# A graph layer's edge MLP: the ring of finished rows and scatter indices goes from four sets to eight

## The chip, the cores and the metric

The kernel runs on one core of a Trainium2 chip. The metric is the time on the device in microseconds (us), the median of several runs; below, a profile of one execution stands beside it. A core has five engines with a queue of instructions each: TensorE (PE in the profile), VectorE (DVE), ScalarE (ACT), GpSimd (POOL) and SyncE (SP). DMAs are issued from the queues of SP and POOL.

## The reference, cut to what matters

Two layers on a graph of 3125 nodes with 256 features. There are 53125 edges, sorted by target: 25000 random pairs in both directions, and one self loop for each node.

```python
h = relu(layernorm(x))
# layer 0: attention with edge features
xn = layernorm(h) * ln_w + ln_b
w_phys = (silu(rbf @ w1 + b1) @ w2 + b2) * cutoff[:, None]     # per edge: 64 -> 256 -> 256
msg_phys = xn[col] * w_phys
Q, K, V = xn @ wq + bq, xn @ wk + bk, xn @ wv + bv             # 8 heads of 32
scores = sum(Q[row] * K[col]) / sqrt(32) * cutoff
attn = softmax(scores, over the 8 heads)
x = x + h + segment_sum(msg_phys + gate * attn * V[col], row) @ wo + bo
# layer 1: graph attention with a softmax over the edges of a node, 4 heads of 64
x = x + gat(relu(layernorm(x)), W, a_l, a_r, src, dst)
```

What the change touches is the line of `w_phys`: an MLP over all edges, in their given order.

## The kernel before, in words

The kernel first counts the edges of each tile of 128 source nodes and works out for every edge its place in an order that groups edges by that tile (`pos_i`, DVE). It also makes the keys, values and normalized rows of the nodes and stores them to memory (`node_kvx`). Then come three long stages: the edge MLP, layer 0 and layer 1.

**The edge MLP** takes the 53125 edges in 104 quads (`QUADS`) of 4 x 128 = 512 edges. For each quad:

- SP has loaded the edge features (L347), one load for four quads.
- PE transposes them (L1170, L1171), and DVE copies the result out of PSUM (L933).
- PE multiplies by w1 (L1236), ACT applies bias and silu (L608), PE multiplies by w2 (L1250).
- DVE writes 4 words of data for each edge (cutoff, source, target, scaled cutoff) into the quad's set of rows `recA` (L940) and adds b2 into the same rows (L944, two halves).
- ACT multiplies the rows by the cutoff (L617, four instructions, "the cut"), and it has earlier copied the four columns of indices for the quad into a set of `idxA` (L599).
- POOL scatters the rows to the memory tensor `sorted_edges` with four indirect DMAs of 128 rows (L474). Only these hold POOL in this stage.

Each engine runs the quads in its own loop (`run`, with an `unroll` of four; `run8` on PE with eight). `run` writes a few turns out in a straight line at the head, then a loop, then a tail. With four steps a turn and a lag of two, the head has 8 quads and the loop 24 turns. Inside a step the engines are shifted: in step n ACT copies the indices of quad n, applies silu to quad n-1 and cuts quad n-2; DVE copies features of quad n and finishes rows of quad n-2; POOL scatters quad n-2.

`recA` and `idxA` are rings of four sets. Quad n uses set n mod 4. Before ACT copies indices into a set (L599), and before DVE writes into it (L940), they wait until the four scatters of quad n-4 have landed, by the semaphores `scattered0` to `scattered3`. The rows of `recA` lie in a shared tensor called `arena`, in columns which the node stage uses before for `kvx_st` (so DVE waits for the stores of `kvx_st` before its MLP loop).

After the last quad DVE adds bo to all of xs in one instruction (L956). SP and POOL wait until all scatters have landed. SP then reads the sorted records (L388), ACT takes the indices out of them (L643), POOL gathers node rows by them (L494), and layer 0 works on groups of 256 edges. Layer 0's own buffers reuse the space: half of the gathered rows lie in the tensor `work`, from column NT * H on. Before the MLP the same columns hold the counting tables `rank` and `oh`, which DVE has read for the last time when it has made `pos_i`.

Of the kernel before, what the change touches and what calls it, by code (L numbers as in the profile page):

```python
# [28 lines left out]
I32 = mybir.dt.int32  # L29

P = 128
# [56 lines left out]
def gnn_kernel(nc, x, src, dst, edge_attr_64, edge_weight, w1, b1, w2, b2, ln_w, ln_b, wq, bq, wk, bk,  # L88
               wv, bv, wo, bo, gate, W, a_l, a_r, out):
    N, H = x.shape  # L90
# [5 lines left out]
    NT = -(-N // P)  # L96
# [6 lines left out]
    QUADS = CC // 4  # L103
# [19 lines left out]
    with ExitStack() as ctx:  # L123
        def sb(name, shape, dt=F32):
            return ctx.enter_context(nc.sbuf_tensor(name, shape, dt))
# [63 lines left out]
        def carve(n):  # L189
            v = arena[:, at[0]:at[0] + n]  # L190
            at[0] += n
            assert at[0] <= arena_n, at[0]
            return v
# [5 lines left out]
        rows_at = at[0]  # L199
        recA = carve(4 * 4 * REC).rearrange("p (s c n) -> p s c n", s=4, c=4)  # L200

# [38 lines left out]

        idxA = sb("idxA", [P, 4, 4], I32)
        idxB = sb("idxB", [P, 8, GJ], I32)
# [29 lines left out]
        def s(name):  # L272
            if name not in S:
                S[name] = sem(name)
            return S[name]
# [28 lines left out]
        def _(sp):  # L304
# [76 lines left out]

            for r in range(4):
                sp.wait_ge(s(f"scattered{r}"), 16 * 4 * (QUADS // 4))

# [33 lines left out]
        def _(pool):  # L418
# [47 lines left out]
            def scatter(st):  # L466
                st = st.back(2)
                if not st.real():
                    return
                pool.wait_ge(s("idxA_ready"), st.n + 1)  # L470
                pool.wait_ge(s("rows_cut"), st.n + 1)
                alone(pool)
                for c in range(4):
                    pool.indirect_dma_start(  # L474
                        rec_dram[:, :], bass.IndirectOffsetOnAxis(ap=idxA[:, st.slot(4), c:c + 1], axis=0),
                        recA[:, st.slot(4), c, :], None, bounds_check=NS - 1, oob_is_err=False).then_inc(
                            s(f"scattered{st.slot(4)}"), 16)

            run(pool, QUADS, 4, 2, scatter)


            for r in range(4):
                pool.wait_ge(s(f"kvx_out{r}"), 16 * ((NT - r + 3) // 4))
            for r in range(4):
                pool.wait_ge(s(f"scattered{r}"), 16 * 4 * (QUADS // 4))

# [70 lines left out]
        def _(act):  # L557
# [37 lines left out]
            def mlp(st):  # L595
                if st.real():
                    if not st.first(4):
                        act.wait_ge(s(f"scattered{st.slot(4)}"), 64 * st.turn(4))
                    act.copy(idxA[:, st.slot(4), :], pos_i[:, bass.ds(st.n * 4, 4)]).then_inc(s("idxA_ready"), 1)  # L599
                c = st.back(2)  # L600
# [9 lines left out]
                if c.real():  # L610

                    act.wait_ge(s("metaA_ready"), c.n + 1)
                    for t in range(2):
                        act.wait_ge(s("recA_ready"), 2 * c.n + t + 1)
                        for i in (2 * t, 2 * t + 1):
                            row = recA[:, c.slot(4), i, :]
                            ins = act.activation(row[:, 0:H], row[:, 0:H], ACT.Copy, scale=row[:, H:H + 1])  # L617
                    ins.then_inc(s("rows_cut"), 1)

            run(act, QUADS, 4, 2, mlp)  # L620


# [158 lines left out]
        def _(dve):  # L781
# [145 lines left out]
            def mlp(st):  # L927
# [8 lines left out]
                if st.real():  # L936
                    r = st.slot(4)
                    if not st.first(4):
                        dve.wait_ge(s(f"scattered{r}"), 64 * st.turn(4))
                    dve.tensor_copy(recA[:, r, :, H:REC], meta_in[:, bass.ds(st.n * 4, 4), :]).then_inc(  # L940
# [9 lines left out]
            for r in range(4):  # L950
                dve.wait_ge(s(f"kvx_out{r}"), 16 * ((NT - r + 3) // 4))
            run(dve, QUADS, 4, 2, mlp)

# [482 lines left out]
```

## Time and profile before

| what | value |
|---|---|
| median of 3 runs | 2514.63 us (2512.04 to 2518.51) |
| the profiled execution, its own time | 2514.38 us |
| its span, first to last instruction | 2512.6 us |
| mean granted clock of TensorE | 0.971 of full speed |
| busy: PE / DVE / ACT / POOL | 2155.4 / 1961.2 / 1689.9 / 1587.8 us |
| scatters of the MLP (L474) | 416, busy 410.4 us |
| gathers of layer 0 (L494) | 464 |
| gathers of layer 1 (L548) | 464 |

The busy time of an engine is a sum over stages that have different limits, so it doesn't say what sets the end of one stage. For that the timeline is read: in it each row gives the start, the duration, the engine, the line, what is written from what, how many instructions stand together, and in brackets how long the engine had been idle before and what released it. "issue" there means that the engine waited for nothing that the profile shows.

### The profile page before, as it was taken

How to read it: one execution, taken by the hardware profiler on the slowest of the kernel's cores; microseconds unless marked ns; L12 is line 12 of the kernel's file. 1: busy time of each engine (PE TensorE's matmuls, PEld its weight loads, DVE VectorE, ACT ScalarE, POOL GpSimd, SP SyncE). 2: the span in 40 equal slices, each digit the busy share in tenths (PEclk: the TensorE clock that was granted, in tenths of full speed). 3: DMA queues.
4: the chain of work that ended last, by engine and by line, in shares of the span. 5: the costliest groups of instructions: out<-in, count | busy, mean ns of one | idle time of the engine just before them, and what ended most of it. 6: DMA issues, size and time to landing. Idle time of an engine off the chain costs nothing.

```text
span 2512.6 us, 62086 instructions
## 1 busy us (share of the span) xinstructions
PE 2155.4 (86%) x14858; PEld 1765.1 (70%) x14859; DVE 1961.2 (78%) x6401; ACT 1689.9 (67%) x6944; POOL 1587.8 (63%) x1700
## 2 busy tenths in 40 slices
PE   0579999999968888888888888869999999999994
PEld 0347777777747777777766776658888888888883
DVE  8983333333338999998989998879999999999998
ACT  2125555555547777777777775558888888888883
POOL 5346777777776565655555563157777777777772
PEclk9999999999989999999999999989999999999997
DMA  7243333333339999989989995123323222223232
GB/s 226 85 175 115 128 126 129 125 129 125 127 124 333 302 306 313 306 301 300 312 290 304 308 310 161 39 74 81 80 78 79 79 78 79 78 79 81 79 78 69
DMA packets 153328, 413.79 MB, mean 165 GB/s; under 512 B 40848, under 2 KB 53045, under 8 KB 153282
## 3 DMA queue, kind: packets, MB, share of 16 engines
q0 software_dynamic: 79360, 301.93, 37.4%
q1 hardware_dynamic: 73922, 111.33, 13.7%
q8 instruction: 18, 0.29, 0.1%
q14 instruction: 28, 0.23, 0.0%
HBM read 328.69 MB, written 84.60 MB: 164 GB/s over the span
## 4 chain that ended last, share of the span: by engine, by line
DVE 36%; issue 20%; DMA 18%; PE 12%; ACT 9%; DVEq 4%; POOL 1%; ACTq 0%; SPq 0%; POOLq 0%
DMA sorted_edges<-arena,idxA 8%; DMA arena<-sorted_edges 8%; DVE gmax L1111 6%; PE ps L1250 4%; ACT arena L617 3%; DVE arena L973 3%; DVE work L1130 2%; ACT arena L608 2%; DVE el L1106 2%; DVE hrmax L1119 2%; DVE sc L987 2%; DVE arena L980 2%; DVE gmax L1083 2%; PE ps L1283 2%; DVEq L286 1%
## 5 line engine op out<-in xcount | busy, mean ns | idle before, releaser
L548 POOL DMA_INDIRECT arena<-node_row,idxB x464 | 454.5, 980 | 209.2 <-issue 103.6
L474 POOL DMA_INDIRECT sorted_edges<-arena,idxA x416 | 410.4, 987 | 148.3 <-issue 147.4
L1361 PE MATMUL ps<-ident_b,arena 128*128 128x128 bf16 x5568 | 390.4, 220 | 53.0 <-DVE gmax L1111 26.8
L944 DVE TENSOR_TENSOR arena<-ps,b_bc 128x512 f32<-128x512 f32 x208 | 143.8, 691 | 354.6 <-PE ps L1250 354.6
L1250 PE MATMUL ps<-w_sb,arena 128*128 128x256 f32 x1664 | 386.9, 386 | 22.1 <-ACT arena L608 18.2
L1361 PEld LDWEIGHTS ps<-ident_b,arena 128*128 128x128 bf16 x5568 | 331.4, 100 | 87.8 <-DVE gmax L1111 31.4
L1250 PEld LDWEIGHTS ps<-w_sb,arena 128*128 128x128 f32 x1664 | 308.3, 190 | 99.8 <-issue 56.2
L494 POOL DMA_INDIRECT work<-node_kvx,idxB x232 | 234.3, 1010 | 165.1 <-issue 52.4
L494 POOL DMA_INDIRECT arena<-node_kvx,idxB x232 | 233.1, 1005 | 166.4 <-issue 53.0
L626 ACT ACTIVATE away<-iota,srcB 128x128 f32<-128x128 f32 x928 | 315.0, 386 | 0.2
L1283 PE MATMUL ps<-arena,work 128*128 128x256 f32 x928 | 252.9, 396 | 58.1 <-issue 52.1
L754 ACT ACTIVATE work<-work,mscale x928 | 247.3, 337 | 26.8 <-DVE work L1130 18.4
L1286 PE MATMUL ps<-arena,work 128*128 128x256 f32 x928 | 245.2, 388 | 0.0
L1397 PE MATMUL ps<-arena,work 128*128 128x260 f32 x928 | 241.8, 382 | 2.3 <-DVE arena L1138 2.3
L1298 PE MATMUL ps<-hq,work 128*128 x928 | 242.9, 385 | 0.0
L1283 PEld LDWEIGHTS ps<-arena,work 128*128 128x128 f32 x928 | 161.4, 194 | 89.1 <-issue 74.2
L633 ACT ACTIVATE work<-away 128x256 f32<-128x256 f32 x464 | 191.1, 412 | 13.7 <-PE ps L1397 1.7
L1170 PE MATMUL ps<-ident,work 128*128 128x128 f32 x489 | 139.6, 286 | 70.7 <-ACT work L633 69.8
L1286 PEld LDWEIGHTS ps<-arena,work 128*128 128x128 f32 x928 | 178.8, 195 | 28.5
L1298 PEld LDWEIGHTS ps<-hq,work 128*128 128x128 f32 x928 | 179.9, 194 | 25.2
L1397 PEld LDWEIGHTS ps<-arena,work 128*128 128x128 f32 x928 | 175.3, 189 | 24.4 <-DVE arena L1138 3.6
L617 ACT ACTIVATE arena<-arena 128x256 f32<-128x256 f32 x416 | 176.7, 501 | 7.2 <-DVE arena L944 7.1
(168 smaller groups left out, 4909.2 us busy)
## 6 DMA issues: line engine op xcount, KB each, us to landing
arena<-sorted_edges SPq DMA_DIRECT2D x232, 260.0 KB, 5.1
arena<-in_edge_attr SPq DMA_DIRECT2D x25, 512.0 KB, 3.6
node_kvx<-arena SPq DMA_DIRECT2D x24, 384.0 KB, 2.3
arena<-node_row,idxB POOLq DMA_INDIRECT x464, 2.8
sorted_edges<-arena,idxA POOLq DMA_INDIRECT x416, 2.4
sorted_edges<-arena SPq DMA_DIRECT2D x25, 260.0 KB, 2.1
sorted_edges<-arena SPq DMA_DIRECT2D x1, 6240.0 KB, 21.1
arena<-node_kvx,idxB POOLq DMA_INDIRECT x232, 5.2
```

Of the source, the lines that this page charges most:

```text
L474: pool.indirect_dma_start(rec_dram[:, :], bass.IndirectOffsetOnAxis(ap=idxA[:, st.slot(4), c:c + 1], axis=0), recA[:, st.slot(4), c, :], N ...
L494: pool.indirect_dma_start(kvx_g(st)[:, j, :], None, kvx_dram[:, :], bass.IndirectOffsetOnAxis(ap=idxB[:, st.slot(8), j:j + 1], axis=0)).th ...
L548: pool.indirect_dma_start(row1_g[:, st.slot(8), j, :], None, row1_dram[:, :], bass.IndirectOffsetOnAxis(ap=idxB[:, st.slot(8), j:j + 1], a ...
L617: ins = act.activation(row[:, 0:H], row[:, 0:H], ACT.Copy, scale=row[:, H:H + 1])
L626: act.activation(away[:, st.slot(2), j, :], iota1[:, :], ACT.Abs, bias=srcB[:, st.slot(8), j:j + 1], scale=-1.0).then_inc(away_ready, 1)
L754: ins = act.activation(v, v, ACT.Copy, scale=mscale[:, d.slot(8), h:h + 1])
L1250: ins = pe.matmul(ps[:, 5 + t, half * H:(half + 1) * H], hidT[:, r, m, half, t * P:(t + 1) * P], w2_sb[:, m, :], start=m == 0, stop=m == 1)
L1283: pe.matmul(ps[:, 3 + r, 0:H], oneh[:, r8, j, :], msgP[:, r, j, :], start=j == 0, stop=False)
L1286: ins = pe.matmul(ps[:, 3 + r, 0:H], oneh[:, r8, j, :], msgA[:, r, j, :], start=False, stop=j == GJ - 1)
L1298: ins = pe.matmul(ps[:, 1 + r, j * H:(j + 1) * H], onehT[:, r, j, :], hq[:, bass.ds(t, 1), :].rearrange("p a n -> p (a n)"), start=True, s ...
L1361: pe.matmul(bank[:, h * P:(h + 1) * P], parts[:, i:i + 1].to_broadcast([P, P]), ident_b[:, :], start=h == 0 and part == 0, stop=False)
L1397: ins = pe.matmul(ps[:, 5 + r, 0:NH1 * HE], oneh[:, r8, j, :], msg1[:, r, j, :], start=j == 0, stop=j == GJ - 1)
```

## The change

The rings of `recA` and `idxA` have eight sets in place of four, and eight semaphores `scattered0` to `scattered7`. The loops of ACT, DVE and POOL over the quads have eight steps a turn in place of four (with the lag of two: 16 quads in the head, 11 turns). `recA` moves to the tensor `work`, from column NT * H on; its old columns in `arena` stay reserved, for what shares them. All instructions of a quad stay the same.

```diff
-        recA = carve(4 * 4 * REC).rearrange("p (s c n) -> p s c n", s=4, c=4)
+        carve(4 * 4 * REC)
+        recA = work[:, NT * H:NT * H + 8 * 4 * REC].rearrange("p (s c n) -> p s c n", s=8, c=4)
...
-        idxA = sb("idxA", [P, 4, 4], I32)
+        idxA = sb("idxA", [P, 8, 4], I32)
...
-            for r in range(4):
-                sp.wait_ge(s(f"scattered{r}"), 16 * 4 * (QUADS // 4))
+            for r in range(8):
+                sp.wait_ge(s(f"scattered{r}"), 16 * 4 * (QUADS // 8))
...
-                        rec_dram[:, :], bass.IndirectOffsetOnAxis(ap=idxA[:, st.slot(4), c:c + 1], axis=0),
-                        recA[:, st.slot(4), c, :], None, bounds_check=NS - 1, oob_is_err=False).then_inc(
-                            s(f"scattered{st.slot(4)}"), 16)
-            run(pool, QUADS, 4, 2, scatter)
+                        rec_dram[:, :], bass.IndirectOffsetOnAxis(ap=idxA[:, st.slot(8), c:c + 1], axis=0),
+                        recA[:, st.slot(8), c, :], None, bounds_check=NS - 1, oob_is_err=False).then_inc(
+                            s(f"scattered{st.slot(8)}"), 16)
+            run(pool, QUADS, 8, 2, scatter)
...
-                    if not st.first(4):
-                        act.wait_ge(s(f"scattered{st.slot(4)}"), 64 * st.turn(4))
-                    act.copy(idxA[:, st.slot(4), :], pos_i[:, bass.ds(st.n * 4, 4)]).then_inc(s("idxA_ready"), 1)
+                    if not st.first(8):
+                        act.wait_ge(s(f"scattered{st.slot(8)}"), 64 * st.turn(8))
+                    act.copy(idxA[:, st.slot(8), :], pos_i[:, bass.ds(st.n * 4, 4)]).then_inc(s("idxA_ready"), 1)
...
-            run(act, QUADS, 4, 2, mlp)
+            run(act, QUADS, 8, 2, mlp)
...
-                    r = st.slot(4)
-                    if not st.first(4):
-                        dve.wait_ge(s(f"scattered{r}"), 64 * st.turn(4))
+                    r = st.slot(8)
+                    if not st.first(8):
+                        dve.wait_ge(s(f"scattered{r}"), 64 * st.turn(8))
...
-            run(dve, QUADS, 4, 2, mlp)
+            run(dve, QUADS, 8, 2, mlp)
```

## Rows read from the trace of the kernel before

**Rows 1.** Timeline, POOL: the first and the last scatter of the MLP stage.
```profile
196.24 1.16 POOL L474 DMA_INDIRECT sorted_edges<-arena,idxA  x1 [11.49 <-issue]
...
742.51 0.97 POOL L474 DMA_INDIRECT sorted_edges<-arena,idxA  x1 [0.31 <-issue]
```

**Rows 2.** Waits, 190 to 745 us: us in total, times, longest us.
```profile
DVE arena L944 <- PE ps L1250: 354.6, 208, 4.0
ACT idxA L599 <- DMA sorted_edges<-arena,idxA: 225.4, 100, 3.7
POOL sorted_edges L474 <- issue: 147.4, 413, 11.5
```

**Rows 3.** Groups of POOL, 196.24 to 743.48 us: busy us, mean ns, idle before.
```profile
L474 POOL DMA_INDIRECT sorted_edges<-arena,idxA x416 | 410.4, 987 | 148.3 <-issue 147.4 <-ACT arena L617 0.3 <-DMA sorted_edges<-arena,idxA 0.3
```

**Rows 4.** Timeline, POOL: first and last of 13 scatters in unbroken sequence.
```profile
235.06 0.97 POOL L474 DMA_INDIRECT sorted_edges<-arena,idxA  x1 [0.30 <-issue]
...
250.41 0.97 POOL L474 DMA_INDIRECT sorted_edges<-arena,idxA  x1 [0.31 <-issue]
```

**Rows 5.** Timeline, ACT and POOL over one turn of the ring.
```profile
296.88 1.69 ACT L617 ACTIVATE arena<-arena 128x256 f32<-128x256 f32 x4
...
298.15 0.97 POOL L474 DMA_INDIRECT sorted_edges<-arena,idxA  x1 [0.30 <-issue]
...
299.44 0.97 POOL L474 DMA_INDIRECT sorted_edges<-arena,idxA  x1 [0.32 <-issue]
...
300.90 0.19 ACT L599 COPY idxA<-pos_i 128x4 int32 x1 [2.33 <-DMA sorted_edges<-arena,idxA]
...
301.02 1.26 ACT L608 ACTIVATE arena<-ps,b_sb 128x512 f32<-128x512 f32 x2
...
302.17 1.69 ACT L617 ACTIVATE arena<-arena 128x256 f32<-128x256 f32 x4
...
303.27 0.97 POOL L474 DMA_INDIRECT sorted_edges<-arena,idxA  x1 [0.30 <-issue]
...
304.73 0.97 POOL L474 DMA_INDIRECT sorted_edges<-arena,idxA  x1 [0.49 <-issue]
```

**Rows 6.** Timeline, POOL: two of three pauses ahead of a quad's second scatter.
```profile
343.85 0.98 POOL L474 DMA_INDIRECT sorted_edges<-arena,idxA  x1 [2.10 <-issue]
...
479.54 0.97 POOL L474 DMA_INDIRECT sorted_edges<-arena,idxA  x1 [1.79 <-issue]
```

**Rows 7.** Timeline, TensorE: transposes of two quads, three quads apart, early in the stage.
```profile
198.20 0.27 PE L1170 MATMUL ps<-ident,arena 128*128 128x128 f32 x1
...
213.00 0.27 PE L1170 MATMUL ps<-ident,arena 128*128 128x128 f32 x1
```

**Rows 8.** Timeline, DVE and POOL around DVE's large add.
```profile
727.96 0.97 POOL L474 DMA_INDIRECT sorted_edges<-arena,idxA  x1 [0.30 <-issue]
728.16 6.82 DVE L956 TENSOR_TENSOR xs<-xs,bo_bc 128x6400 f32<-128x6400 f32 x1
...
729.24 6.58 POOL L474 DMA_INDIRECT sorted_edges<-arena,idxA  x1 [0.31 <-ACT arena L617]
736.12 0.97 POOL L474 DMA_INDIRECT sorted_edges<-arena,idxA  x1 [0.30 <-issue]
```

**Rows 9.** Timeline, DVE and POOL: a copy of edge data over a scatter's start.
```profile
209.21 0.22 DVE L940 COPY arena<-arena 128x16 f32<-128x16 f32 x1
...
209.22 0.97 POOL L474 DMA_INDIRECT sorted_edges<-arena,idxA  x1 [0.30 <-issue]
```

**Rows 10.** Timeline, from the last scatter into layer 0.
```profile
744.97 3.67 SPq L388 DMA_DIRECT2D arena<-sorted_edges  x8
...
748.82 0.98 POOL L494 DMA_INDIRECT arena<-node_kvx,idxB  x1 [5.34 <-ACT idxB L643]
...
755.16 0.69 DVE L973 TENSOR_TENSOR arena<-ps,arena 128x512 f32<-128x512 f32 x1 [20.19 <-DMA arena<-node_kvx,idxB]
```

**Rows 11.** DMA queues, 263 to 695 us: packets, MB, share of 16 engines.
```profile
q8 instruction: 1, 0.02, 0.0%
```

More of the change, by code:

```diff
@@ L474, in scatter @@
                     pool.indirect_dma_start(
-                        rec_dram[:, :], bass.IndirectOffsetOnAxis(ap=idxA[:, st.slot(4), c:c + 1], axis=0),
-                        recA[:, st.slot(4), c, :], None, bounds_check=NS - 1, oob_is_err=False).then_inc(
-                            s(f"scattered{st.slot(4)}"), 16)
-            run(pool, QUADS, 4, 2, scatter)
+                        rec_dram[:, :], bass.IndirectOffsetOnAxis(ap=idxA[:, st.slot(8), c:c + 1], axis=0),
+                        recA[:, st.slot(8), c, :], None, bounds_check=NS - 1, oob_is_err=False).then_inc(
+                            s(f"scattered{st.slot(8)}"), 16)
+            run(pool, QUADS, 8, 2, scatter)
             for r in range(4):
                 pool.wait_ge(s(f"kvx_out{r}"), 16 * ((NT - r + 3) // 4))
-            for r in range(4):
-                pool.wait_ge(s(f"scattered{r}"), 16 * 4 * (QUADS // 4))
+            for r in range(8):
+                pool.wait_ge(s(f"scattered{r}"), 16 * 4 * (QUADS // 8))
             def gather0(st):
@@ L615, in mlp @@
                         for i in (2 * t, 2 * t + 1):
-                            row = recA[:, c.slot(4), i, :]
+                            row = recA[:, c.slot(8), i, :]
                             ins = act.activation(row[:, 0:H], row[:, 0:H], ACT.Copy, scale=row[:, H:H + 1])
                     ins.then_inc(s("rows_cut"), 1)
-            run(act, QUADS, 4, 2, mlp)
+            run(act, QUADS, 8, 2, mlp)
             def one_hot_away(st, src_ready, away_ready):
```

## The prediction

> **What bounds the kernel now.** I read the page first: no engine is saturated over the span, so the change has to be judged in its own stage. That stage is the edge MLP: 104 quads of 512 edges, each scattered to memory by four POOL DMAs. Its first scatter starts at 196.24 us and its last at 742.51 [rows 1]: 546.27 us, or 5.25 us a quad, of a span of 2512.6.
>
> Then the view of waits over the stage [rows 2]. It is tempting: ACT waits 225.4 us for scatters to land before it overwrites a set of indices (L599), and DVE waits 354.6 us for TensorE. This doesn't say what a larger ring is worth, because an engine off the path may wait for free. So next the groups and the timeline of POOL. Its 416 scatters are busy 410.4 us, 987 ns each, and idle 148.3 us before them, nearly all put down to "issue" [rows 3]. The timeline shows what that issue is: from 235.06 to 250.41 us twelve scatters follow each other, 15.35 / 12 = 1.279 us apart, 0.97 busy and 0.30 between, and nobody is waited for [rows 4]. Four of them make 5.12 us a quad. POOL is thus already at its own pace for most of the stage; only 5.25 - 5.12 = 0.13 us a quad is anything else.
>
> What the ring costs is seen in one turn of it [rows 5]. The fourth scatter of a quad starts at 298.15; ACT's index copy, which waits for it to land, starts at 300.90, 2.75 us later. The cut of the rows (L617) then starts at 302.17 and ends 1.69 later, at 303.86, and POOL's next quad starts 0.87 us after that end, at 304.73. POOL had been free at 303.27 + 0.97 = 304.24 and could have started at 304.54; it lost 0.18 us. One quad earlier the cut ended at 296.88 + 1.69 = 298.57 and POOL went on at 299.44, the normal 1.29 after its scatter before: just in time. The loop scatter, landing, index copy, silu, cut, scatter closes with almost no slack, and loses mostly once in four quads, where ACT begins a new turn of its loop.
>
> **The change part by part.**
>
> 1. The waits on scattered sets reach back eight quads where they reached back four (ACT's L599, DVE's L940). What goes is the lateness of POOL's quad starts. By subtraction: 415 intervals at 1.279 are 530.79 us; the stage has 546.27, so 15.48 us are not pace. Of these, three pauses of POOL (343.85, 479.54 [rows 6], and one like the first at 615.26) are 1.79 + 1.48 + 1.80 = 5.07 us. All three fall on the second scatter of a quad, where POOL waits for nothing: the ring has no part in them and they stay. One scatter beside DVE's large add takes 5.60 us too long (part 3). The first two scatters are 0.20 late while starting up. What is left is 15.48 - 5.07 - 5.60 - 0.20 = 4.61 us. Added up by themselves, the 22 quad starts later by 0.10 us or more come to 4.9. I take 4.8 us of gain; the bounds are 4.6 and 5.3 (the latter if the pace is 1.2775, what scatters within a quad often have).
>
> 2. What is late next. POOL must never starve. TensorE, while the ring does not hold it, starts a quad's transposes at 198.20 and the third one after it at 213.00: 14.80 / 3 = 4.93 us a quad [rows 7]. ACT is busy 0.19 + 1.26 + 1.70 = 3.15 us a quad [rows 5], DVE less. So the producers gain 5.12 - 4.93 = 0.19 us a quad on POOL, and 1.8 more in each pause. At the end they would be about 104 x 0.19 + 5 = 25 us ahead; eight sets allow some 20 (eight quads of 5.12, less two which lie between the index copy and the cut, the landing and the way from copy to scatter). The ring gates the producers again near the end, POOL never. Cost of this: nothing. If that cover fails and TensorE sets the pace, it is still faster than POOL.
>
> 3. The end of the stage. DVE's add of bo to xs (L956, 6.82 us) starts when DVE has made its last rows. Now that is at 728.16, and the scatter that starts at 729.24 takes 6.58 us, ending at 735.82, 0.84 after the add's end at 734.98; the scatter at 727.96 was not touched [rows 8]. I read this as: a scatter needs something that the add holds about 0.97 - 0.84 = 0.13 us after its start; the loss was 5.61, the least there can be for this add being 6.82 - 1.28 = 5.54 (it began just after such a point) and the most 6.82. After the change DVE is done some 10 to 20 us before POOL's end rather than a quad or two, but POOL still has scatters to issue, so the block stays. Its phase becomes a matter of chance: mean (5.54 + 6.82) / 2 = 6.18, a loss of 0.57 against now, between 0 and 1.2. On this the Trainium skill, SBUF — State Buffer, section "Who interferes with whom", bears: a tensor_tensor with both inputs in SBUF blocks GpSimd's reads, but, as it infers, not its descriptor writing. If an issue needed only the write side the add would be no cause, its new place would cost nothing, and the sum would be -4.8; the row shows an issue that ends right behind the add, and I go by the row (the reading of the indices could be what is blocked).
>
> 4. DVE's small copy of the edge data (L940, 0.17 us, SBUF to SBUF) now drifts past POOL's starts instead of staying clear of them. At 209.21 one lay over a scatter's start at 209.22, and the scatter took its 0.97 [rows 9]: 0 us, at most 104 x 0.17 x 0.17 / 1.28 / 2 = 1.2 us, if each overlap delayed POOL. I take 0.1.
>
> 5. The loops of POOL, ACT and DVE have bodies of 8 quads, straight parts of 16 instead of 8, and 11 turns instead of 24 [(104 - 16) / 8]. On ACT and DVE any cost of a turn lies under the lead from part 2. On POOL the turn shows nothing now (its intervals there are 1.28), and the longer body has twice the scatters: taken as 0. The other bound is in the rivals. Four more semaphores to wait for on SP and POOL after the stage: a few tenths at most, taken as 0.1.
>
> 6. The new place of the rows (in the work tensor, free since the positions are made) and the larger idxA: same instructions, same sizes, same memory; 0.
>
> What follows the last scatter hangs on POOL alone: SP reads the first records at 744.97, POOL gathers from 748.82, DVE works from 755.16 after 20.19 us of idling [rows 10]. So what POOL gains passes on whole, and layers 0 and 1 move earlier unchanged.
>
> Sum: -4.8 + 0.6 + 0.1 + 0.1 = -4.0 us. The profiled execution took 2514.38 us (span 2512.6 and 1.8 around it); its median of runs is 2514.63, 0.25 more. 2514.38 - 4.0 = 2510.4; against the median 2510.6. I forecast **2510.6 us**, 0.16% less.
>
> **Rivals.**
>
> A, TensorE's pace: the 225 us that ACT waits are real and the stage falls to 4.93 us a quad. Then 104 x (5.25 - 4.93) = 33 us go, 2481 us. For it: the size of the waits [rows 2]. Against it: POOL's spacing, the same with and without a wait behind it [rows 4]; it would need that spacing to be a result of the ring. Chance 0.06.
>
> B, nothing comes back: the late quad starts are not the ring's but those of ACT's turn, and return with eight sets at every eighth quad, or new pauses of POOL take the place. 2514.6, or half of it (2512.5). For it: the lateness sits at one place of the loop. Against it: the producers' lead, once there, covers 0.2 us easily. Chance 0.14.
>
> C, slower: POOL's own loop turn stalls, because its body has doubled. POOL has no slack, so each turn counts in full. The nearest row for a stall of POOL that nobody causes is 2.10 - 0.30 = 1.80 us [rows 6]; 11 turns give 19.8, with the -4.0 a net of +15.8: 2530 us. It decides for "slower" from (7.5 + 4.0) / 11 = 1.05 us a turn. Against it: from 263 to 695 us, over 80 quads, one instruction block of 0.02 MB was loaded in all [rows 11], so loops are not loaded anew at each turn. The Trainium skill, Runtime: NRT & Kernel Launch, section "Instruction fetch mechanics", speaks against the change here: a taken branch to a page that is not in the engine's small window waits for a fetch. By that rule C comes if POOL's longer body leaves the window; the row shows no such reload with bodies of four quads, and no run yet with eight. Chance 0.06.
>
> **How the numbers follow.** The forecast has 0.74, A 0.06, B 0.14, C 0.06. A change of under 0.3% (7.5 us) is about what a measurement of this kernel can't tell from none. The forecast's own spread is 2509.6 to 2511.8 from the bounds, but the runs of before lie from 2512.04 to 2518.51, so a median of few runs moves by 2 to 3 us, and the layers after can shift as much. Range: 2505 to 2518, which holds the forecast and B and leaves out A and C and the far ends of the noise. Faster by over 0.3% (under 2507.1): A, and about one in seven of the forecast, 0.16. Slower (over 2522.2): C and a little noise, 0.07. Same: 0.77.
>
> **What would show it.** Right: first to last scatter near 541.5 to 542 us (546.27 now); no quad start of POOL over 1.30 us but the three pauses; ACT's wait for scatters falling from 225 us to well under 100 and TensorE's quads 4.93 apart at first; one scatter of 6.4 to 7.7 us under the add, which starts before 722; the time from last scatter to the first gather unchanged (6.3 us). Wrong: spacing under 1.27 (A), late starts at every eighth quad (B), pauses of over 1 us at POOL's loop turns (C).

## The result, and the profile after

| | median | lowest to highest | runs |
|---|---|---|---|
| kernel before | 2513.53 us | 2504.47 to 2528.52 | 18 |
| kernel after | 2499.19 us | 2491.78 to 2510.28 | 18 |

The ratio is 0.994, with a 95% interval of 0.9924 to 0.9956: 14 to 15 us faster. Forecast were 4 us and 2510.6. The sign of the sum was right and its size was not, and the time lies below the range of 2505 to 2518. In some sets below one or two executions took over 3200 us; no median and no ratio here counts them.

The profiled execution of after took 2496.66 us, its span is 2494.8 and the mean granted clock of TensorE 0.968. Against the profile of before the span is 17.8 us shorter. These 17.8 us lie as follows:

| stretch | before | after | difference |
|---|---|---|---|
| start to first scatter | 196.2 | 193.9 | -2.3 |
| first to last scatter (start to start) | 546.3 | 536.5 | -9.8 |
| last scatter to the end | 1770.0 | 1764.3 | -5.7 |

In the last stretch layer 0, from its first to its last gather, took 788.0 us where it took 792.2. Instructions of the scatter's line are now L475; each line behind `carve` has moved down by one.

The engines' busy times, from the page of after:
```profile
PE 2150.6 (86%) x14858; PEld 1763.6 (71%) x14859; DVE 1964.8 (79%) x6401; ACT 1704.3 (68%) x6944; POOL 1582.5 (63%) x1700
```
They are within 15 us of those before (PE 2155.4, DVE 1961.2, ACT 1689.9, POOL 1587.8), so the work is the same and what has changed is when it is done.

First POOL, as in [rows 1, 3, 10]: the first and the last scatter of after and the first gather of layer 0 (start, duration).
```profile
193.94 1.16 POOL L475 DMA_INDIRECT sorted_edges<-work,idxA  x1 [10.76 <-issue]
...
730.46 0.97 POOL L475 DMA_INDIRECT sorted_edges<-work,idxA  x1 [0.30 <-issue]
736.80 0.98 POOL L495 DMA_INDIRECT arena<-node_kvx,idxB  x1 [5.38 <-ACT idxB L644]
```

and its group, from the page of after (busy, mean ns, idle before):
```profile
L475 POOL DMA_INDIRECT sorted_edges<-work,idxA x416 | 411.0, 988 | 137.3 <-issue 135.4
```
The scatters are as long as before (988 ns each, 987 before), so the whole gain of the stage is idle time: 148.3 us before, 137.3 now (0.7 of these 11 us lie ahead of the first scatter, which waited 11.49 and now 10.76).

The waits of the stage in after, 190 to 735 us, as in [rows 2] (us in total, times, longest):
```profile
DVE work L945 <- PE ps L1251: 323.2, 208, 3.3
ACT work L618 <- DVE work L945: 192.5, 207, 1.4
POOL sorted_edges L475 <- issue: 135.4, 410, 10.8
...
ACT idxA L600 <- DMA sorted_edges<-work,idxA: 2.0, 3, 1.0
```
ACT's wait for scatters has gone from 225.4 us to 2.0. What came of it is under a tenth of that: the 9.8 us of the stage.

The place of the first pause, [rows 6]: scatter 113 (counted from 0) started there at 343.85 after 2.10 us of idle time. In after scatter 113 starts at 338.60, and the whole neighbourhood runs at one pace:
```profile
334.77 0.97 POOL L475 DMA_INDIRECT sorted_edges<-work,idxA  x1 [0.31 <-issue]
...
337.32 0.97 POOL L475 DMA_INDIRECT sorted_edges<-work,idxA  x1 [0.30 <-issue]
338.60 0.98 POOL L475 DMA_INDIRECT sorted_edges<-work,idxA  x1 [0.30 <-issue]
339.89 0.97 POOL L475 DMA_INDIRECT sorted_edges<-work,idxA  x1 [0.30 <-issue]
```
Behind the very first scatter, no interval of the stage is over its pace but one, that of the scatter under the large add. All three pauses are gone, and with them every late quad start. The pace is taken as 530.46 us for the stage, 415 intervals of 1.2782: that is what the run early_bo8 below took, which has neither late starts nor pauses nor a long scatter. In the profile of before the 15.8 us beyond it (546.28 less 530.46) were late starts 4.80, pauses 5.07, the long scatter 5.60, and some 0.35 of rest. In after they are 0, 0, 5.70 and 0.36. The stage's difference is so 4.80 + 5.07 - 0.10 = 9.77 us, as measured (9.76). The term that the prediction lacked is that of the pauses.

### The profile page after: what moved, and what is told of

The parts are those of the page before. It is cut to its first block, busy times and chain, and to the rows that moved or that the text cites. A ratio compares the mean times of both kernels' runs of the same rounds, so it can differ in the third digit from the quotient of the medians.

```text
span 2494.8 us, 61930 instructions
## 1 busy us (share of the span) xinstructions
PE 2150.6 (86%) x14858; PEld 1763.6 (71%) x14859; DVE 1964.8 (79%) x6401; ACT 1704.3 (68%) x6944; POOL 1582.5 (63%) x1700
## 4 chain that ended last, share of the span: by engine, by line
DVE 37%; PE 23%; issue 18%; DMA 9%; POOL 4%; DVEq 4%; ACT 3%; SPq 0%; POOLq 0%; ACTq 0%
PE ps L1251 12%; DMA arena<-sorted_edges 7%; DVE gmax L1112 5%; POOL sorted_edges L475 4%; PE ps L1237 4%; DVE arena L974 3%; DVE work L1131 2%; DVE sc L988 2%; DVE el L1107 2%; DVE hrmax L1120 2%; DVE arena L981 2%; PE ps L1284 2%; PE ps L1287 2%; DVE gmax L1084 2%; DVE work L846 1%
## 5 line engine op out<-in xcount | busy, mean ns | idle before, releaser
L475 POOL DMA_INDIRECT sorted_edges<-work,idxA x416 | 411.0, 988 | 137.3 <-issue 135.4
L945 DVE TENSOR_TENSOR work<-ps,b_bc 128x512 f32<-128x512 f32 x208 | 143.9, 692 | 323.2 <-PE ps L1251 323.2
L618 ACT ACTIVATE work<-work 128x256 f32<-128x256 f32 x416 | 188.7, 500 | 192.5 <-DVE work L945 192.5
```

The lines of the kernel that those rows point to most:

```text
L475: pool.indirect_dma_start(rec_dram[:, :], bass.IndirectOffsetOnAxis(ap=idxA[:, st.slot(8), c:c + 1], axis=0), recA[:, st.slot(8), c, :], N ...
```

## Why the pauses went: what was asked of the chip

Two accounts stood against each other, and a third came from the trace.

- The prediction's: the pauses belong to POOL and not to the ring. Then something else in the change removed them: the longer loop, the eight semaphores or the new place of the rows.
- The ring's: they need the deeper ring.
- Theory Q, from the trace. POOL's records show one small MOVE (29 ns) in its sequencer (POOLq) for each scatter, on the scatter's line and ahead of it. This stream has holes in which no MOVE comes and for which no wait stands. What a hole costs depends on how far the stream had run ahead, and that depends on the ring.

The records on which Q rests are one line's instructions over a short window, in before (duration, first and last start). The sequencer's MOVE stands still from 340.5 to 343.6; the scatter at 343.85 with its pause comes right behind it.
```profile
L474 POOLq MOVE  x2: 29/29/29, 340.5 to 343.6; - x2
L474 POOL DMA_INDIRECT sorted_edges<-arena,idxA x1: 973/973/973, 340.8 to 340.8; - x1
```
The same in after. The hole is there too, 2.70 us from 331.6 to 334.3, and three scatters start in and around it as if nothing had happened:
```profile
L475 POOL DMA_INDIRECT sorted_edges<-work,idxA x3: 972/973/974, 330.9 to 333.5; - x3
L475 POOLq MOVE  x2: 29/29/29, 331.6 to 334.3; - x2
```

Over the whole stage I paired the n-th MOVE with the n-th scatter and took the time between the two starts, the lead. In before its median is 2.24 us and after a hole 1.5 is left; in after the median is 11.56 us and after a hole at least 5.6 is left.

### First set: on a chip where the kernel before takes 2783 us

Four kernels: the kernel before and the one after, once more with profiles on one chip; the eight-set kernel with its waits four quads back; and the kernel before with loops of eight quads alone. The first two have no edit.

> The kernel before once more, for a second profile. Theory P (the three pauses of POOL of 1.5 to 1.8 us ahead of the scatters 113, 217 and 321 belong to this kernel): they stand at the same three scatters, the stage from first to last scatter takes 546 to 547 us. Rival R (a pause is an accident of one execution and as likely in either kernel): other places or another number of pauses. Layer 0 and layer 1 show by how much they differ between executions of the same code (805.9 us from the first gather to DVE's last product in layer 0 in the first profile, 801.8 in the kernel with eight sets). Ratio 1.000.

> The kernel with eight sets once more. First to last scatter 536.5 us again (415 x 1.279 + 5.7 under DVE's add). Theory P: no pause in the stage. Rival R: up to three pauses, then 538 to 542 us. Theory S (the part of the 14 us gain that lies outside the MLP stage is real): layer 0 near 802 us again. Its rival (layer 0 only varies): anywhere from 800 to 808. Ratio 0.994.

wait4, against the eight-set kernel, on ACT and in the same way on DVE:
```diff
-                    if not st.first(8):
-                        act.wait_ge(s(f"scattered{st.slot(8)}"), 64 * st.turn(8))
+                    if not st.first(4):
+                        o = st.back(4)
+                        act.wait_ge(s(f"scattered{o.slot(8)}"), 64 * o.turn(8) + 64)
```


> Eight sets in the work tensor and loops of eight quads, but ACT and DVE wait for the scatters of the quad four back, as in the kernel before. It undoes the ring's depth alone. If the depth is the whole cause: late quad starts return, about 4 to 5 us, the pauses return by theory P, stage 543 to 547 us, ratio 0.999 to 1.000. If the place of the rows or the loop form carries the gain: the stage stays near 537 us and the ratio at 0.994.

loop8, against the kernel before, for pool, act and dve:
```diff
-            run(pool, QUADS, 4, 2, scatter)
+            run(pool, QUADS, 8, 2, scatter)
```


> Ring of four sets in its old place, but the loops of ACT, DVE and POOL have eight quads a turn. It does the loop form alone. If the late starts come from ACT's loop turn and the ring only lets them through: they are halved (2.4 us instead of 4.8), stage 544 us, ratio 0.999. If the loop form matters not at all: 546 us, 1.000. If the loop form is what takes the pauses away: about 539 us, 0.997.

| | median us | ratio to before | 95% | stage in the profile |
|---|---|---|---|---|
| c_before | 2783.95 | 1.0007 | 0.9984 to 1.0030 | 685.83 |
| c_after | 2782.92 | 1.0008 | 0.9984 to 1.0032 | 678.37 |
| wait4 | 2780.59 | 1.0006 | 0.9982 to 1.0029 | 687.34 |
| loop8 | 2784.30 | 1.0013 | 0.9993 to 1.0032 | 683.55 |

All four are the same here, and neither the stages nor the ratios came out as expected: the chip has another limit. In c_before the longest waits of the stage (190 to 880 us) are other ones than in [rows 2]:
```profile
DVE arena L944 <- remote: 223.4, 33, 10.8
...
ACT idxA L599 <- DMA sorted_edges<-arena,idxA: 173.1, 71, 4.6
...
PEld ps L1250 <- DVE arena L944: 101.8, 32, 5.4
```
And in its timeline DVE stands still for 10.79 us ahead of an add of b2, released by nothing that the profile names ("remote"); TensorE waits 4.94 us for that add, and POOL pauses for 5.37:
```profile
262.66 1.29 DVE L944 TENSOR_TENSOR arena<-ps,b_bc 128x512 f32<-128x512 f32 x2 [10.79 <-remote]
263.40 6.39 PE L1250 MATMUL ps<-w_sb,arena 128*128 128x256 f32 x16 [4.94 <-DVE arena L944]
...
265.96 0.97 POOL L474 DMA_INDIRECT sorted_edges<-arena,idxA  x1 [5.37 <-issue]
```
The stage is 140 us longer than on the chip before. The expectations of later sets speak of holes in the queues of all engines; the rows say less: DVE's adds start late, 223.4 us in 33 waits, and TensorE's long waits are for DVE. Why DVE is late isn't shown. The deeper ring takes 7 us off the stage in the profile (685.83 to 678.37), but the ratio doesn't show it.

On the pauses this set does say something. Two of them are there in c_after, with its eight sets: 1.43 us at scatter 113 and 1.25 at 377. And loop8, with four, has none at 113. This is c_after at scatter 113, first the scatter in the timeline, then the hole in the records of its line:
```profile
376.44 0.98 POOL L475 DMA_INDIRECT sorted_edges<-work,idxA  x1 [1.74 <-issue]
...
L475 POOLq MOVE  x2: 29/29/29, 373.5 to 376.2; - x2
```
POOL's stream had run less far ahead here: its median lead in c_after is 2.54 us, not 11.56. So eight sets as such don't remove a pause; that speaks against the plain account of the ring and for Q.

### Second set: on a chip where the kernel before takes 2515 us

The same edits again, and one that tests the prediction's part 3. In early_bo8 the add of bo is done in two parts ahead of the last quads: 16 of the 25 node tiles before DVE's MLP loop, the other 9 in its third step.
```diff
+                if st.first(3) and st.u == 2:
+                    dve.tensor_tensor(xs[:, 16:NT, :], xs[:, 16:NT, :],
+                                      bo_bc[:, :].unsqueeze(1).to_broadcast([P, NT - 16, H]), ALU.add).then_inc(s("xhb"), 1)
...
+            dve.tensor_tensor(xs[:, 0:16, :], xs[:, 0:16, :],
+                              bo_bc[:, :].unsqueeze(1).to_broadcast([P, 16 - 0, H]), ALU.add).then_inc(s("xhb"), 1)
...
-            dve.tensor_tensor(xs[:, :, :], xs[:, :, :], bo_bc[:, :].unsqueeze(1).to_broadcast([P, NT, H]),
-                              ALU.add).then_inc(s("xhb"), 1)
...
-            dve.wait_ge(s("xhb"), 1)
+            dve.wait_ge(s("xhb"), 2)
```


> The kernel before again, since in the runs just made it took 2783 us where it had taken 2514, and its stage 685.8 us, with holes of 2.5 to 5.5 us in the queues of all engines. If those holes belong to the chip and not to the kernel, then on a chip where it takes about 2514 us the stage is 546 us again, with POOL as its bound; theory P then wants the three pauses at the scatters 113, 217 and 321 (the one at 113 was also there in the disturbed executions of both kernels, which speaks for a cause in POOL's own count), rival R wants them elsewhere or not at all. Ratio 1.000.

> Eight sets and loops of eight, waits reaching four quads back: undoes the depth alone. On a chip where the kernel before takes 2514 us: depth as the cause gives a stage of 543 to 547 us and a ratio near 1.000; place or loop form as the cause gives 537 us and 0.994.

> Ring of four in its old place, loops of eight quads. On a chip where the kernel before takes 2514 us: late quad starts at every eighth quad instead of every fourth, 2.4 us less, stage 544 us, ratio 0.999, if they come from ACT's loop turn; unchanged at 546 us and 1.000 if not.

> The kernel with eight sets, with DVE's add of bo to xs (6.8 us beside POOL's scatters) moved ahead of the MLP in two pieces, where POOL issues nothing. My theory (the add holds a scatter up until it ends): no scatter over 1.2 us, stage 531 us instead of 536.5, so 5.7 us less than the kernel with eight sets, a ratio of 0.992 where that has 0.994. Rival, by the inference of the Trainium skill (SBUF — State Buffer, section Who interferes with whom) that such an add does not block descriptor writing: a scatter of 6.7 us remains at some place of the stage, the ratio 0.994.

| | median us | ratio to before | 95% | stage | late starts | pauses at scatter: us |
|---|---|---|---|---|---|---|
| d_before | 2514.68 | 0.9990 | 0.9975 to 1.0004 | 549.34 | 5.92 | 113: 1.79, 217: 1.61, 321: 1.79 |
| d_wait4 | 2507.69 | 0.9972 | 0.9956 to 0.9988 | 546.47 | 4.09 | 113: 1.43, 201: 1.34, 289: 1.41, 377: 0.63 |
| d_loop8 | 2509.76 | 0.9982 | 0.9967 to 0.9997 | 548.20 | 6.18 | 113: 1.79, 217: 1.55, 321: 1.79 |
| early_bo8 | 2493.08 | 0.9911 | 0.9891 to 0.9932 | 530.46 | 0 | none |

The late starts are summed over the quads that start 0.10 us or more behind POOL's pace; the stage is in us, first to last scatter. The first pause is there in each kernel of this set whose waits reach four quads back, and in a repetition of the kernel before it is at the same scatter, 344.27 where [rows 6] has 343.85; so it is no accident of one execution:
```profile
344.27 0.98 POOL L474 DMA_INDIRECT sorted_edges<-arena,idxA  x1 [2.10 <-issue]
```
d_wait4 has all of the change but the depth of the waits: memory, indices, loops, semaphores. Its stage is as long as before and it has four pauses, of which this is the second (timeline of POOL):
```profile
453.49 0.98 POOL L475 DMA_INDIRECT sorted_edges<-work,idxA  x1 [0.30 <-issue]
456.11 0.97 POOL L475 DMA_INDIRECT sorted_edges<-work,idxA  x1 [1.64 <-issue]
```
Its wait of ACT for scatters, over the stage:
```profile
ACT idxA L601 <- DMA sorted_edges<-work,idxA: 225.9, 100, 3.5
```
It is as long as before too. So the 10 us of the stage, against after, hang on the depth alone. By the device time the depth is worth 0.9972 less 0.9940, some 8 us. The other 0.28%, which d_wait4 has against before with waits four back, isn't the ring's: between the profiles of d_before and d_wait4 2.9 us of it lie in the stage (1.8 of them in late starts) and 4.0 in layer 0 (787.5 us after 791.5). See the end of this section.

d_loop8 answers what its expectation asked of the late starts. Its loops turn half as often, and it has 23 late starts where before has 22, still mostly one in four quads. So it isn't ACT's loop turn that makes them late, as the prediction had read in [rows 5]; what sets their place wasn't found.

early_bo8 shows both halves of the add away from the stage's end, and POOL without a long scatter:
```profile
178.88 4.42 DVE L954 TENSOR_TENSOR xs<-xs,bo_bc 128x4096 f32<-128x4096 f32 x1
...
187.19 2.55 DVE L937 TENSOR_TENSOR xs<-xs,bo_bc 128x2304 f32<-128x2304 f32 x1
...
725.43 0.97 POOL L475 DMA_INDIRECT sorted_edges<-work,idxA  x1 [0.31 <-issue]
731.88 0.98 POOL L495 DMA_INDIRECT arena<-node_kvx,idxB  x1 [5.47 <-ACT idxB L644]
```
530.46 us are 415 intervals of 1.278 us: the stage is at POOL's pace from end to end. The gain over after is 6.06 us in the stage; the ratios, 0.9911 here and 0.9935 to 0.9940 for the change alone, differ by 6 to 7 us, though their intervals still overlap. This is the fastest version, 2493.08 us.

### Third set: on a chip where the kernel before takes 2829 us

Which single part moves the pauses, and how deep must the ring be? wait5 is wait4 with 5 in place of 4: `if not st.first(5)`, `o = st.back(5)`. sem8 is the kernel before with its four sets and its place, but loops of eight and eight semaphores, with wait4's waits. placeidx is the kernel before with rows and indices in their new memory:
```diff
-        recA = carve(4 * 4 * REC).rearrange("p (s c n) -> p s c n", s=4, c=4)
+        carve(4 * 4 * REC)
+        recA = work[:, NT * H:NT * H + 4 * 4 * REC].rearrange("p (s c n) -> p s c n", s=4, c=4)
...
-        idxA = sb("idxA", [P, 4, 4], I32)
+        idxA = sb("idxA", [P, 8, 4], I32)
```
early_bo4 is the kernel before with early_bo8's edit.

> Eight sets in memory, waits reaching five quads back: one set more than before in use. The trace of the kernel with eight sets shows that POOL's instruction stream has its hole of 2.7 us at scatter 113 there too, but four scatters were queued already and cover it. Theory Q (depth lets the stream run ahead, which takes away both the late starts and the pauses): one more set lets it run ahead by up to one quad, 5.1 us, more than the hole takes, so both go; stage 537 to 538 us, ratio 0.994. Rival (the pauses go with a depth of eight alone, or by the loop form): late starts gone, pauses of 1.2 to 1.8 us left, stage 540 to 542 us.

> Ring of four sets in its old place, but eight semaphores in turn, loops of eight quads, waits four quads back. Against the form of the kernel before it changes the number of semaphores and the loops alone. Stage 546 us by every theory. The form with eight sets in memory and the same waits had its stage at 546.5 us too, but a ratio of 0.9972, with layer 0 at 787.5 us from first to last gather, against 791.5 to 794.4 in three executions with four sets. If the semaphores do that: layer 0 near 788 and ratio near 0.998; also pauses at the scatters 113, 201, 289 instead of 113, 217, 321. If it is the place of the rows or of what lies behind the indices: layer 0 near 792 and ratio 0.999 to 1.000.

> The kernel before with its four sets of rows in the work tensor, and the index tensor allocated with eight sets of which four are used, so that all that lies behind it moves by 64 bytes. Loops, semaphores and waits as before. Stage 546 us, pauses at 113, 217, 321. If place is what shortens layer 0: layer 0 near 788 us, ratio near 0.998. If not: near 792 us and 1.000. A third possibility is that layer 0 only varies by 5 us between builds.

> The kernel before with DVE's add of bo moved ahead of the MLP. The long scatter goes: 5.6 to 6.3 us less, stage 540 to 543 us, ratio 0.9978 to 0.9985, late starts and the three pauses left as they are. If with a ring of four the freed time were lost again to the ring: stage 546 us.

| | median us | ratio to before | 95% | stage |
|---|---|---|---|---|
| wait5 | 2822.50 | 0.9986 | 0.9963 to 1.0009 | 698.76 |
| sem8 | 2825.35 | 0.9987 | 0.9965 to 1.0009 | 702.27 |
| placeidx | 2825.55 | 0.9998 | 0.9979 to 1.0017 | 706.78 |
| early_bo4 | 2818.08 | 0.9971 | 0.9949 to 0.9993 | 704.46 |

This chip is slow in the way of the first one, and again three kernels can't be told apart from the kernel before. wait5, of which no pause was expected, has two here, at scatters 113 and 377, each behind a quad that started late. Only early_bo4 stands out: its add is out of POOL's way and it has no long scatter, 0.29% with an interval that ends at 0.9993. That points to a price of the long scatter with a ring of four as well; its stage, 704.46, is no proof of it beside 702.27 in sem8.

### Fourth set: on a chip where the kernel before takes 2518 us

> The kernel with eight sets once more, beside the three below. On a chip where the kernel before takes about 2515 us: stage 536.5 us, no pause (theory Q: the hole of POOL's instruction stream at scatter 113 lies under queued scatters), layer 0 from first to last gather near 788 us if the part of the gain outside the stage belongs to the build, 788 to 794 if it only varies. Ratio 0.994. On a chip with holes in all queues, where the kernel before takes 2780 us or more, no difference beyond 0.3%: there TensorE's and DVE's own holes make the quads late, which a deeper ring behind them can't mend.

> Waits reaching five quads back. On a chip where the kernel before takes about 2515 us: theory Q gives no late start, no pause, stage 537 to 538 us, ratio 0.994. Rival (the pauses need the full depth): pauses left, stage 540 to 542 us, ratio 0.996.

> Ring of four, eight semaphores, loops of eight. On a chip where the kernel before takes about 2515 us: stage 546 to 548 us; layer 0 near 788 and ratio 0.997 to 0.998 if number of semaphores or loop form carry the part outside the stage, 792 and 1.000 if the place does. The pauses at 113, 201, 289, 377 if their spacing follows the number of semaphores.

> Four sets in the work tensor, index tensor of eight sets, all else as before. On a chip where the kernel before takes about 2515 us: layer 0 near 788 and ratio 0.998 if the place carries the part outside the stage, else 792 and 1.000; pauses at 113, 217, 321.

| | median us | ratio to before | 95% | stage | late starts | pauses at scatter: us |
|---|---|---|---|---|---|---|
| f_after | 2501.99 | 0.9935 | 0.9911 to 0.9960 | 536.51 | 0 | none |
| f_wait5 | 2500.63 | 0.9939 | 0.9919 to 0.9959 | 536.18 | 0 | none |
| f_sem8 | 2515.63 | 0.9993 | 0.9978 to 1.0009 | 546.88 | 4.71 | 113: 1.25, 201: 1.31, 289: 1.41, 377: 0.54 |
| f_placeidx | 2519.43 | 1.0005 | 0.9987 to 1.0022 | 550.79 | 8.30 | 113: 1.80, 217: 1.33, 321: 1.79 |

This set decides. Place and larger index tensor: nothing that can be measured. Eight semaphores and loops of eight with a ring of four: nothing in time, but the later pauses move, from every 104th scatter to every 88th. One of them, scatter 289 of f_sem8:
```profile
572.57 0.97 POOL L474 DMA_INDIRECT sorted_edges<-arena,idxA  x1 [1.72 <-issue]
```
One set more than four in use, f_wait5, brings the whole gain of eight. In its stage:
```profile
L475 POOL DMA_INDIRECT sorted_edges<-work,idxA x416 | 410.6, 987 | 137.4 <-issue 136.2 <-ACT idxA L601 0.6 <-DMA sorted_edges<-work,idxA 0.6
```
And yet ACT still waits 173.7 us for scatters there:
```profile
ACT idxA L601 <- DMA sorted_edges<-work,idxA: 173.7, 86, 3.2
```
173.7 of 225.4 us of waiting stay and all the time that the ring cost is gone. The total of a wait says nothing of its price.

What the stream of MOVEs shows over the ten kernels profiled on the quicker chips (2514 to 2518 us for the kernel before):

| kernels | hole of | spacing of holes | median lead | left after a hole | pauses |
|---|---|---|---|---|---|
| before, d_before, d_loop8, f_placeidx | 3.08 us | 104 scatters | 2.24 us | 1.5 us | 3 |
| d_wait4, f_sem8 | 2.70 us | 88 | 2.24 us | 1.5 us | 4 |
| f_wait5 | 2.70 us | 88 | 6.58 us | 5.2 us | none |
| after, f_after, early_bo8 | 2.70 us | 88 | 11.4 to 11.6 us | 5.5 to 14.2 us | none |

Each kernel has its holes at fixed scatters, the first always between the MOVEs of scatters 113 and 114. None has lost them; they cost only where the stream was close to the scatters. How close can be put in a rule and tried on all 18 profiles, those of the slower chips too, which have 64 holes. The scatter before the hole sets when the next would start at its pace, 1.278 us later. A scatter whose MOVE is the last before a hole starts either then or 0.22 us after the hole's end, whichever is later. This gives all 64 starts to 0.01 us: 38 with a pause and 26 without. For before at scatter 113: 340.78 + 1.28 = 342.06 by its pace, and 343.63 + 0.22 = 343.85 by the hole; it started at 343.85. For after: the hole ended at 334.29, and its pace was 338.60. The holes without a pause include six in kernels with waits four back and two in c_after, all on the slower chips, where the MOVE before the hole happened to be 3.1 us or more ahead of its scatter's pace; in the 38 with a pause it was 2.6 us or less. So what the hole costs is set by the lead, and the ring only through it.

With four sets the next quad's rows are ready just when they are wanted (part 1 of the prediction saw this in [rows 5]), so the stream can't go ahead: it has to wait for them. With a fifth set ACT is a quad further and the stream with it. The prediction's account falls: on the quicker chips no other part of the change removes a pause, the depth alone does. What I varied is the depth; that it works through the lead is read from the records, and the 64 holes bear it out.

What stays open. Outside the stage, 3 us or so of the 14 to 15 aren't accounted for. The six kernels with waits four back have stages of 548.0 us on the mean, the three with deeper waits and the late add 536.4: 11.6 us, a ratio of 0.9954, just inside the measured interval. The rest lies in other stages or in chance: layer 0 took 783.2 us in f_sem8, which has a ring of four, 798.4 in f_placeidx, and 795.5 in f_after, which has eight. That spread doesn't follow the edit, and one profile of each can't say what it follows. Nor is it known why d_wait4 was 0.28% faster than before, when its parts measured 0.9993 (f_sem8) and 1.0005 (f_placeidx).

## Why the prediction was wrong, by its own steps

**What bounds the kernel now: right.** POOL's pace sets the stage, and 225 us of ACT's waiting were no 225 us of time. Rival A expected a spacing under 1.27 us; it is 1.278 in every kernel, with 12 scatters queued or with one.

**Part 1, the late quad starts: right in size.** Forecast 4.8 us, measured 4.80 to 0. What it said of their place, ACT's loop turn, d_loop8 doesn't bear out (see there).

**Part 1, the pauses: this step failed.** It said: "All three fall on the second scatter of a quad, where POOL waits for nothing: the ring has no part in them and they stay." The first half is what the rows show. The second doesn't follow. That POOL waits for nothing tells who doesn't hold the scatter; it doesn't tell what its own sequencer had been able to prepare. The pause is the end of a 3.08 us hole in that sequencer's stream, and the ring had kept the stream's lead at 2.24 us. The sequencer's records were in the trace of before, and the prediction read the scatters alone. With the pauses the sum is -4.8 - 5.1 + 0.6 + 0.1 + 0.1 = -9.1, and the stage gave 9.8. The 0.7 between them is 0.5 for the scatter under the add, which lost 0.1 more than before and not 0.6, and the small terms. So the pauses are 5.1 of the 10.3 us by which the forecast fell short; 4.6 lie outside the stage (nearer 3 if the mean stages above are taken), where the prediction put 0.1 and no run here shows a cause.

**Part 2: right that nothing else becomes late.** TensorE's transposes of two quads three apart, as in [rows 7], are 14.80 / 3 = 4.93 us a quad apart in after too, and the producers were done 32 us before the last scatter. Part 2 had put their lead at 20 to 25 us and part 3 at 10 to 20; and the ring gates them less than it said, since ACT waits 2.0 us for scatters in the whole stage. None of this costs time.
```profile
195.90 0.27 PE L1171 MATMUL ps<-ident,arena 128*128 128x128 f32 x1
...
210.70 0.27 PE L1171 MATMUL ps<-ident,arena 128*128 128x128 f32 x1
```

**Part 3: right.** The block stays; forecast was a loss of 5.54 to 6.82 us under an add that begins before 722.
```profile
697.92 0.97 POOL L475 DMA_INDIRECT sorted_edges<-work,idxA  x1 [0.30 <-issue]
698.21 6.82 DVE L957 TENSOR_TENSOR xs<-xs,bo_bc 128x6400 f32<-128x6400 f32 x1
...
699.20 6.68 POOL L475 DMA_INDIRECT sorted_edges<-work,idxA  x1 [0.30 <-issue]
706.18 0.97 POOL L475 DMA_INDIRECT sorted_edges<-work,idxA  x1 [0.30 <-issue]
```
The scatter is 5.70 us too long and ends 0.85 behind the add (0.84 before). The stream's lead of 15.6 us doesn't help it, since here the scatter itself is held and not its stream. In the sum the term stood at its mean, 0.6 us more than before, and came out at 0.1; over the nine kernels of the quicker chips that have the late add the loss is 5.49 to 6.63 us, so which value comes is chance, as the prediction said. f_wait5 has it at another place, 712.60, and with the same price:
```profile
712.60 6.70 POOL L475 DMA_INDIRECT sorted_edges<-work,idxA  x1 [0.30 <-issue]
```
early_bo8 removed it, so what was a reading of one row is now shown for this add: a tensor_tensor of 128x6400 with both inputs in SBUF holds up an indirect DMA of POOL. That agrees with the rule that was weighed, the Trainium skill, SBUF — State Buffer, section "Who interferes with whom", so far as it speaks of GpSimd's reads; its inference that descriptor writing isn't blocked would have left the scatter at 0.97 us, and the runs are against that being all that an issue needs.

**Parts 4 to 6: right at their sizes.** No interval beyond pace is left for the small copies, the longer loops or the new place; the new place with the larger index tensor measured 1.0005 (f_placeidx), longer loops with eight semaphores 0.9993 (f_sem8). From the last scatter to the first gather it is 6.34 us after 6.31, so the four more semaphores cost nothing there (0.1 was forecast), and what POOL gained passes on whole, as was forecast. Only d_loop8, at 0.9982 with an interval that ends at 0.9997, hints at a gain from the loops alone; its stage is no shorter (548.20) and f_sem8, which has the same loops, doesn't repeat it.

**Rivals.** B expected the late starts to return at every eighth quad; none did. C expected pauses at POOL's loop turns; there is none in after, whose 11 turns run at 1.278 us a scatter, but for the one under the add. On C the prediction set the Trainium skill, Runtime: NRT & Kernel Launch, section "Instruction fetch mechanics", beside it: if a longer body left the window, each turn would pay. No turn does, with a body of eight quads; whether that body lies in the window no run here shows.

**The range.** Its lower end lacked the case that happened, because the pauses had been taken out of every case. 5.07 us that "stay" were a term with no bound of its own. Had they stood with a bound, from 0 to -5.07, the low end would have reached 2500, and the measured 2499.2 would still have lain just outside.

## What to carry to other kernels

A pause of an engine that "waits for nothing" may be a gap in its instruction stream, and its price is what of the gap the engine's queued lead doesn't cover; so look at what the sequencer had done ahead, and ask whether a ring keeps it short. For a ring that closes just in time, try one set more before doubling it: here five sets gave all of what eight gave. And look for the one long scatter or load beside a large SBUF-to-SBUF vector instruction, and move that instruction to where the DMA-issuing engine isn't the bound: 6 us of this stage for moving one add.

## What the runs showed of the hardware

- POOL's sequencer runs ahead of its indirect DMAs, to a limit: in after no lead is over 15.64 us but under the add, and from about scatter 272 on the longest lead of nearly every quad is 15.62, some 12 scatters of 1.278 us. The ring isn't what holds it there, since ACT waits 2.0 us for scatters in all.
- A hole of that stream holds a scatter until 0.22 us after its end, if the scatter hasn't started by then (64 holes, to 0.01 us).
- The stream has holes that belong to no wait: 3.08 us every 104 scatters in kernels with four semaphores, 2.70 us every 88 in those with eight. Loops of eight alone (d_loop8) leave 104 and 3.08. Only the semaphores differ on POOL between d_loop8 and f_sem8 (104 and 88). What a hole is, and why semaphores set its spacing, wasn't found. The loading of instructions doesn't fit them: the instruction queues of the DMA view, 263 to 695 us, show 1 packet in before [rows 11] and 3 in after (packets, MB, share); from 255 to 655 us they show none in either, and three holes of each kernel lie there.
```profile
q8 instruction: 2, 0.03, 0.0%
q14 instruction: 1, 0.01, 0.0%
```
- The same program takes 2515 us on some chips and 2783 or 2829 on others, 11 to 12% more. On the first of these DVE's adds start late, with waits of up to 10.8 us for nothing that the profile names, and a change worth 0.6% on the quicker chips can't be told from none (c_after: 1.0008, 0.9984 to 1.0032). The clock of TensorE is too near to be the cause: 0.955 granted on the mean in c_before against 0.971 in before, 1.6% for 11%.
